# State-space layer: the pairwise differences of the running sums, all on VectorE before, now split by heads between VectorE and ScalarE

## The reference, cut to what matters

```
dt = jax.nn.softplus(dt_raw + dt_bias)
dA = jnp.exp(-jnp.exp(A_log) * dt)
dtx = dt[..., None] * xh
...
def step(h, inp):
    dA_t, dtx_t, B_t, C_t = inp
    h = h * dA_t[:, :, None, None] + dtx_t[..., None] * B_t[:, :, None, :]
    y_t = jnp.einsum('bhpn,bhn->bhp', h, C_t)
    return (h, y_t)
```

## Time and profile before

| | before |
|---|---|
| median of 3 runs | 3316.36 us (3308.28 to 3322.06) |
| profiled execution | 3312.32 us, span 3310.2 us |
| TensorE busy, share of span | 81% |
| VectorE busy | 51% |
| ScalarE busy | 42% |
| GpSimd busy | 14% |
| mean granted clock of TensorE | 0.872 |

### The profile page before, as it was taken

How to read it: one execution, slowest core, us unless ns; L and a number is a source line. 1 busy time by engine, 2 the same in 40 slices (tenths; PEclk the granted TensorE clock), 3 DMA queues, 4 the chain that set the end, 5 groups by cost and what they waited for, 6 DMA issues and landing times. The chain is left out here.

```text
span 3310.2 us, 33970 instructions
## 1 busy us (share of the span) xinstructions
PE 2674.6 (81%) x12536; PEld 1656.6 (50%) x12536; DVE 1684.8 (51%) x3451; ACT 1378.1 (42%) x1853; POOL 459.3 (14%) x411
## 2 busy tenths in 40 slices
PE   2888888865888888879994887784688888887998
PEld 1656666542333333355562545453366666665655
DVE  3455555534556665616432778785544444532222
ACT  2333333311555555612223565551366666661121
POOL 0111111110000000000463132232201111000000
PEclk9788888876999999969896989987799989997999
DMA  2000000005333332140246111111200000001000
GB/s 66 7 13 13 13 13 13 7 7 140 54 59 61 63 66 52 27 139 4 52 64 136 52 52 65 39 69 44 57 13 26 26 26 26 13 7 64 13 19 20
DMA packets 126037, 140.94 MB, mean 43 GB/s; under 512 B 38752, under 2 KB 108656, under 8 KB 125872
## 3 DMA queue, kind: packets, MB, share of 16 engines
q1 hardware_dynamic: 113968, 124.07, 13.9%
q0 software_dynamic: 11904, 14.69, 2.7%
HBM read 77.89 MB, written 35.39 MB: 34 GB/s over the span
## 5 line engine op out<-in xcount | busy, mean ns | idle before, releaser
L929 DVE TENSOR_REDUCE xattn_tops<-region 128x2 f32<-128x1024 f32 x256 | 305.6, 1219 | 146.1 <-PE region L735 146.0
L867 ACT ACTIVATE xattn_probs<-region 128x1024 f32<-128x1024 f32 x256 | 256.1, 1022 | 154.1 <-PE region L724 153.3
L2107 PE MATMUL region<-psi_fT 128*128 128x512 f32 x512 | 245.5, 624 | 21.7 <-DVE psi_low L2341 21.1
L122 PE MATMUL region<-gla_xT,weights_even 128*128 128x512 f32 (+1 forms) x416 | 221.0, 687 | 26.7 <-ACT gla_xT L214 26.7
L724 PE MATMUL region<-xattn_qs,xattn_ks 49*128 49x512 f32 x512 | 125.6, 492 | 85.9 <-DVE xattn_tops L929 54.8
L122 PE MATMUL region<-mamba_xT,weights_odd 128*128 128x512 f32 x320 | 169.5, 681 | 5.1 <-DVE mamba_xh L1904 5.1
L2107 PEld LDWEIGHTS region<-psi_fT 128*128 128x128 f32 x512 | 97.1, 200 | 125.4 <-issue 100.6
L122 PEld LDWEIGHTS region<-gla_xT,weights_even 128*128 128x128 f32 (+1 forms) x416 | 82.8, 208 | 151.0 <-issue 119.3
L2128 PE MATMUL region<-psi_ctxv,psi_pT 128*128 128x65 f32 x1024 | 137.4, 300 | 20.8 <-issue 19.4
L2128 PEld LDWEIGHTS region<-psi_ctxv,psi_pT 128*128 128x128 f32 x1024 | 136.3, 216 | 30.0 <-issue 30.0
L751 PE MATMUL region<-xattn_probs,xattn_va 128*32 128x512 f32 x1024 | 144.0, 630 | 1.1 <-ACT xattn_o_T L895 1.1
(11 more groups left out here) (493 smaller groups left out, 5430.4 us busy)
## 6 DMA issues: line engine op xcount, KB each, us to landing
weights_even<-mamba_cs SPq DMA_DIRECT2D x32, 512.0 KB, 4.8
xattn_qs<-xattn_qhi SPq DMA_DIRECT2D x128, 64.0 KB, 2.3
xattn_ks<-xattn_khi SPq DMA_DIRECT2D x128, 64.0 KB, 2.3
moe_sums<-moe_picked SPq DMA_DIRECT2D x9, 512.0 KB, 7.8
gla_x<-in_x SPq DMA_DIRECT2D x8, 512.0 KB, 3.8
x_after_gla<-gla_res SPq DMA_DIRECT2D x8, 512.0 KB, 2.9
xattn_ctxT<-in_ctxT SPq DMA_DIRECT2D x8, 512.0 KB, 4.1
xattn_x<-x_after_gla SPq DMA_DIRECT2D x8, 512.0 KB, 4.1
```

The source lines that it names most:

```text
L122: last = st.nc.tensor.matmul(o[0:m, i, :], w[:, c, col + i * P:col + i * P + m], rhs[:, c, :], start=c == 0, stop=c == kc - 1)
L867: A_(probs[:, p % 3, a, :, :], st.region(f"k{v}")[:], ACT.Exp).then_inc(st.emptying(f"k{v}"), 1)
L929: V.tensor_reduce(tops[:, n % 2, t, a::2], st.region(f"q{u}")[:], AX, ALU.max).then_inc(st.emptying(f"q{u}"), 1)
L2107: last = mm(o[:, a, :], fT[:, h, 0, t * P:t * P + P], fT[:, h, 1 + a, :], start=True, stop=True)
```

## The change

For the second head of each pair the differences are computed by ScalarE, with the opposite sign: Relu(cs - inter) = -min(inter - cs, 0), from four ACTIVATEs of 128x128 whose bias is a column of cs and whose scale is -1. The exponential of `intra` is cut in two, one for each head, the second with scale -1. VectorE does four tiles of a pair where it did eight. ScalarE now waits for the fetch, for the running sums and for "y" of the sequence before, as VectorE did and does; after its own tiles it waits for them (new semaphore "less"), and then for VectorE's.

```
@@ scalar, spread
+    act.wait_ge(st.sem(f"spread{i}"), 16 * (b + 1))
+    act.wait_ge(*st.emptied(f"cs{b}"))
+    if b:
+        act.wait_ge(*st.full(f"y{b - 1}_{i // 2}"))
+    h = 2 * i + 1
+    for t in range(NT):
+        last = A_(intra[:, h, t * P:t * P + P], inter[:, h, t * P:t * P + P], ACT.Relu, scale=-1.0,
+                  bias=Z["cs"][:, t * MH + h:t * MH + h + 1])
+    last.then_inc(st.sem("less"), 1)
+    act.wait_ge(st.sem("less"), MF * b + i + 1)
     act.wait_ge(st.sem("differences"), MF * b + i + 1)
     A_(inter[:, two, :], inter[:, two, :], ACT.Exp).then_inc(st.sem("decayed"), 1)
-    A_(intra[:, two, :], intra[:, two, :], ACT.Exp).then_inc(st.sem("decay"), 1)
+    A_(intra[:, h - 1, :], intra[:, h - 1, :], ACT.Exp)
+    A_(intra[:, h, :], intra[:, h, :], ACT.Exp, scale=-1.0).then_inc(st.sem("decay"), 1)
@@ vector, spread
-    for h in (2 * i, 2 * i + 1):
+    for h in (2 * i,):
         for t in range(NT):
             last = TS(intra[:, h, t * P:t * P + P], inter[:, h, t * P:t * P + P],
                       Z["cs"][:, t * MH + h:t * MH + h + 1], 0.0, ALU.subtract, ALU.min)
```

## The result

The changed kernel takes 3350.46 us (median of 4 runs, 3346.86 to 3352.62), beside 3318.02 us (3308.28 to 3322.06) for the kernel before, measured beside it: ratio 1.0103, 95% interval 1.0084 to 1.0123. It is slower, by 1%. The span of the profiled execution grew from 3310.2 to 3344.6 us, by 34.4.

A forecast was written before the change was run, and what follows sets the result against it. ScalarE's chain to pair 3's first exponential was taken to bound the layer's stretch, then VectorE. Seven sequences at 4.63 us (32.4) plus 3.4 in the last gave 35.8; 3312.3 + 35.8 = 3348 us, range 3332 to 3366.

The forecast's parts named there:

- Which engine sets the stretch: State-space layer: ScalarE to pair 3's first exponential sets the pace, then VectorE; VectorE's 5.03 us idle waits for tile_decay.
- pair 0's share: Pair 0, where ScalarE waits for differences: the exception where VectorE's saving of 0.785 us a pair counts.
- The Relu tile: ScalarE's 128x128 Relu with one bias column: 388 ns, bounds 277 to 480; four tiles take 1.28 us.
- Release: Between one instruction's end and the start of the one waiting for it: about 0.03 us.
- Halves, load, logarithm: Exponential of intra in halves: +0.10 us a pair; pair 0's exposed load: net +0.52; pair 2, behind logarithm: +1.29.
- The sum: Delay up to pair 3's first exponential: 4.63 us a sequence, 3.4 in the last, 35.8 in all.
- the rival with a drain: Pair 0's newly exposed table load also needs a drain: 1.4 us there, 11 over eight sequences, 3359 us; chance 0.07.
- The clock rival: TensorE's low clock lasts 4.6 us longer, into the matmuls of "y": up to 2.3 us a sequence, 3366; chance 0.05.
- VectorE's idle time before the state sum: Sign in the changed profile, at line 1894: grown from 5.03 to about 12.7 us.

The follow-up runs named there:

- f1: Kernel before, with ScalarE's four exponentials of intra moved behind the fourth exponential of inter, nothing added or left out; 3301.3 us, ratio 0.9953.
- f4: f1 plus ScalarE's "xs" part moved behind pair 3, and the last normalisation's statistics moved behind pair 3's differences; 3289.18 us, ratio 0.991.

## Why the prediction was right

It said 3348 us, range 3332 to 3366, slower with 0.88; measured 3350.46. That the two lie 2.5 us apart is partly luck: the forecast adds 35.8 us to the one profiled execution, the medians differ by 32.4, and single runs scatter by some 6 us. The mechanism is what can be judged closely. By the prediction's own steps:

- *Which engine sets the stretch.* ScalarE to the exponential of pair 3, then VectorE. Shown from both sides: relief of VectorE alone returned 0.785 of 3.1 us, exactly pair 0's share; four tiles ahead of pair 3 alone cost 1.30 us of 1.31; work moved behind that exponential came off the time. The wait that the profile gave to nobody was tile_decay's, as its new name for it shows.
- *The Relu tile.* 388 ns taken, 388 measured over 128 tiles. Four tiles took 1.26 us (1.28), eight 2.44 (2.47): overlap is 0.10 us a tile, not 0.09.
- *Release.* 0.03 us held between ScalarE's tiles and its exponential (2036.21 + 1.26 to 2037.50). The load of pair 0 started 0.07 to 0.09 us after VectorE's fourth tile in seven sequences and 0.36 in the one shown above (2031.68 + 0.87 to 2032.91), where 0.03 was taken. That sequence is therefore late by 4.89 us at its state sum and not by 4.6.
- *Halves, load, logarithm.* 0.52 us from half to half; pair 0's loss with the halves, alone, was 0.64 against 0.62 worked out (0.52 + 0.10).
- *The sum.* 4.63 us a sequence against 4.60 in the undisturbed periods. By pairs, from output sum 1902.23 on: +0.56, +1.38, +1.28, +1.38, where +0.52, +1.41, +1.29, +1.41 were worked out. Then 3.4 in the last against 3.1 (52.59 to 55.72 us); 35.8 in all against 35.1 in the layer and 34.4 in the span.
- *No drain.* The exponential starts 0.01 us after the load's end (2032.91 + 1.28 to 2034.20), so the rival with a drain is out, in pair 0 too. The clock rival as well, for the time from state sum to output sum did not grow (41.39 us against 41.40). The granted clock was 0.50 and 0.72 where it had been 0.70 and 0.62, after 12.53 us without work instead of 7.64, and again 1.00 in the stretch after, where "y" runs; the 0.83 ahead of it is a mix of 1.00 up to 2042.50, while TensorE works, and 0.61 in the 12.5 us after it, in which it has nothing to do.
- *A small miss.* VectorE's idle time before the state sum was to be 12.7 us and is 10.56. The rest lies before the shift (1.87) and before "dt" (0.43), 12.9 together. The shift waits because its reciprocal root stands on GpSimd behind the copy of pair 1, which now comes later, and "dt" waits for TensorE's projection; the prediction had followed VectorE's own order only.

In the follow-ups the expectations for f1 and f4 were 0.5 and 1.4 us a period too low. In f1, and in f4 for 0.6 us, it is the wait of ScalarE in pair 1 (0.83 us), which appears once the exponentials of `intra` are out of the way and had not been carried on to the logarithm. The rest in f4, 0.66 us, was lost behind the door.

## What to carry to other kernels

Ask of a piece of work not which engine has more room over the span but which one is waited for in the stretch where the work runs: VectorE was busy 51% and ScalarE 42%, and yet at this door ScalarE had 1.1 us of room and VectorE 5. When the same engine does both what is waited for and what is not, put the first ahead: the order alone was worth 0.75% here, and only afterwards did moving a share of the tiles pay, sized to the idle time and placed in it. Look also at what a new wait pulls behind it; a table load that ran under cover stood bare for 1.3 us each time, of which the earlier differences had paid for 0.785.

## What the runs showed of the hardware beyond what was expected

Some of VectorE's operations, the state product and the shift among them (two inputs in SBUF), take longer beside GpSimd's products, and the rows read as if the two engines took turns, instruction by instruction. In f4_stats_behind the state product (128x512, line 1887) takes 1.69 us at 2016.78, where a product of GpSimd had begun 0.13 us before it and ended at 2017.92; it takes 0.69 us at 2019.81, while GpSimd does its small root steps. The shift of 128x4, 0.15 us elsewhere, ends at 2024.65 after 1.23 us, where the product that GpSimd had begun at 2022.91 ends at 2024.63. It is not that VectorE is always slowed. In one sequence of f1_inter_first both start at 2093.14, and there VectorE's is as short as without company:

```profile
2093.14 0.68 DVE L1886 TENSOR_TENSOR mamba_states<-mamba_states,mamba_eend 128x512 f32<-128x512 f32 x1
```

GpSimd's product takes 1.82 us in its place, and 1.26 the one before it (2091.91), which had begun ahead of VectorE's operation. VectorE's sums with an input in PSUM (line 1889, `states` plus a region) take 0.69 us in the middle of GpSimd's products. So the cost of VectorE work that is moved out of an idle place into the 12 us of GpSimd's products is by these rows (an estimate) its own time and what is left of the product that it meets: 0.69 + 1.14 against 1.69 measured, 0.15 + 1.21 against 1.23. No run was made to test this by itself: it is read from rows, and GpSimd's durations are rough. Open too is the table load that started 0.36 us after its release in one sequence and 0.07 to 0.09 in the others.
